# Two heads' scores in the two halves of TensorE's rows, in a macaron block of FFN, ALiBi attention and FFN

## What is computed

```python
def _L0_attn_ref(q, Wq, Wk, Wv, Wo, bo):       # q: 8 x 512 x 256, H = 16 heads of D = 16
    qh, kh, vh = (proj(q, Wq), proj(q, Wk), proj(q, Wv))
    bias = (-slopes)[:, None, None] * abs(pos[None, :] - pos[:, None])
    scores = einsum('bhld,bhsd->bhls', qh, kh) * D ** -0.5 + bias
    attn = softmax(scores, axis=-1)
    out = einsum('bhls,bhsd->bhld', attn, vh)
    return out @ Wo.T + bo
x = x + 0.5 * _L0_ffn_ref(_layernorm(x), ...)
x = x + _L0_attn_ref(_layernorm(x), ...)
x = x + 0.5 * _L0_ffn_ref(_layernorm(x), ...)
```

## Time and profile before

| | |
|---|---|
| Three runs | 908.52, 913.72, 915.49 us; median 913.72 |
| The profiled execution | 917.76 us, of it 915.9 us from first to last instruction |
| Busy (share of the span) | PE 845.7 us (92%), DVE 652.6 (71%), ACT 527.4 (58%), POOL 426.9 (47%) |
| Mean granted TensorE clock | 0.932 |

### The profile page before, as it was taken

One profiled execution on the slowest core, in us unless ns is written; L12 is line 12 of the kernel. 1 busy time (PEld: TensorE's weight loads), 2 busy tenths in 40 slices (PEclk: granted clock), 3 DMA queues, 4 the chain that ended last, 5 costly groups with the idle time before them and its releaser, 6 DMA issues.

```text
span 915.9 us, 15958 instructions
## 1 busy us (share of the span) xinstructions
PE 845.7 (92%) x4672; PEld 578.9 (63%) x4672; DVE 652.6 (71%) x1359; ACT 527.4 (58%) x745; POOL 426.9 (47%) x486
## 2 busy tenths in 40 slices
PE   3899898959999999999999999999999988999988
PEld 2788787835555665665665665665664447888877
DVE  5788777676677677677677677677678706677774
ACT  4444433505668668668668668668666674344443
POOL 0444433522635645645645645645644455334443
PEclk9999999966999999999999999999998998999999
DMA  9220000274382472472472572472572000010001
GB/s 381 82 64 5 0 0 2 48 198 125 86 226 59 117 208 48 114 208 47 117 205 47 116 206 47 119 203 47 122 200 48 2 2 1 25 46 23 23 23 48
DMA packets 37032, 84.48 MB, mean 92 GB/s; under 512 B 3746, under 2 KB 4770, under 8 KB 36818
## 3 DMA queue, kind: packets, MB, share of 16 engines
q1 hardware_dynamic: 36482, 83.45, 34.1%
q10 hardware_dynamic: 512, 0.53, 0.2%
HBM read 45.68 MB, written 38.87 MB: 92 GB/s over the span
## 4 chain that ended last, share of the span: by engine, by line
PE 74%; DVE 10%; issue 6%; DMA 4%; ACT 2%; POOL 2%; ACTq 0%; DVEq 0%; SPq 0%; POOLq 0%
PE ps L969 68%; DVE row_max L882 4%; DMA q_aug<-max_row 3%; DVE xn L731 2%; PE ps L1020 2%; PE ps L981 2%; PE ps L1025 2%; DVE hid L782 1%; POOL hid_r L488 1%; PE ps L1006 1%; PE ps L1030 1%; ACT gated L590 1%; DMA k_aug<-parts_scratch 1%; DMA parts_scratch<-parts 1%; DVE w_max L839 1%
## 5 line engine op out<-in xcount | busy, mean ns | idle before, releaser
L882 DVE TENSOR_REDUCE row_max<-ps 128x1 f32<-128x512 f32 x512 | 341.6, 688 | 130.1 <-PE ps L969 128.4
L678 ACT ACTIVATE probs<-ps 128x1024 f32<-128x1024 f32 x256 | 252.6, 1022 | 101.4 <-PE ps L969 92.3
L555 POOL TENSOR_TENSOR probs<-probs,diag 128x256 f32<-128x256 f32 x256 | 188.1, 737 | 235.2 <-ACT probs L678 234.9
L969 PE MATMUL ps<-k_aug,q_aug 96*128 96x512 f32 x512 | 222.2, 459 | 13.6 <-DVE row_max L882 6.6
L488 POOL TENSOR_TENSOR hid_r<-hid,hid_r 128x512 fp32r<-128x512 f32 x96 | 124.1, 1294 | 184.0 <-ACT hid_r L584 174.5
L969 PE MATMUL ps<-xnt,wgu_r 128*128 128x512 f32 x768 | 183.0, 396 | 11.4 <-issue 9.2
L969 PEld LDWEIGHTS ps<-k_aug,q_aug 96*128 96x128 f32 x512 | 96.2, 195 | 150.3 <-DVE row_max L882 125.2
L969 PEld LDWEIGHTS ps<-xnt,wgu_r 128*128 128x128 f32 x768 | 144.7, 191 | 44.2 <-issue 10.8
L969 PE MATMUL ps<-q_aug,k_aug 98*128 98x512 f32 x512 | 160.0, 406 | 6.7 <-DMA q_aug<-max_row 6.7
L969 PE MATMUL ps<-probs,v_aug 128*32 128x512 f32 x1024 | 142.2, 629 | 0.8 <-POOL probs L555 0.8
L590 ACT ACTIVATE gated<-ps 128x512 f32<-128x512 f32 x96 | 57.6, 600 | 120.4 <-PE ps L969 120.4
(11 more groups left out here) (62 smaller groups left out, 689.7 us busy)
## 6 DMA issues: line engine op xcount, KB each, us to landing
parts_scratch<-parts SPq DMA_DIRECT2D x128, 256.0 KB, 5.8
q_aug<-parts_scratch SPq DMA_DIRECT2D x32, 512.0 KB, 4.8
k_aug<-parts_scratch SPq DMA_DIRECT2D x32, 512.0 KB, 6.5
x_sb<-x_in SPq DMA_DIRECT2D x8, 512.0 KB, 12.6
x_out<-x_sb SPq DMA_DIRECT2D x8, 512.0 KB, 2.6
wgu_i<-w_gate_up SPq DMA_DIRECT2D x2, 768.0 KB, 6.0
k_aug<-k_rows_scratch SPq DMA_DIRECT2D x1, 1088.0 KB
w_att<-w_att SPq DMA_DIRECT2D x1, 1024.0 KB, 11.1
```

The lines of the kernel that those rows point to most:

```text
L555: nc.gpsimd.tensor_tensor(tile, tile, diag[:, n * QH + 2 * pair:n * QH + 2 * pair + 2, :], ALU.mult).then_inc(fixed, 1)
L678: nc.scalar.activation(probs[:, kt % 2, 2 * pair:2 * pair + 2, :], ps[:, at:at + 2, :], ACT.Exp).then_inc(exp_done, 1)
L882: nc.vector.reduce_max(row_max[:, quad % 2, u % TT, u // TT:u // TT + 1], max_bank(b, tile)[0], mybir.AxisListType.X).then_inc(s1_used, 1)
L969: return nc.tensor.matmul(out, lhs, rhs, start=start, stop=stop, **k)
```

## The change

The bias gets six segments instead of eight (twelve pieces of 42 or 43 tokens, two to a segment, its centre between them), products of parts are three instead of four, and slopes are divided by a unit that leaves powers of two (the exponential's scale and the scale of Q carry the unit), so that no bias row needs a low part. A score contracts 62 rows (60 in the first pass). Heads are laid in pairs: `q_aug` and `k_aug` have head i of a pair at partitions 64i to 64i+61. Two successive matmuls of a pair then stand in rows 0 to 63 and 64 to 127 of the array and write different PSUM banks. The first pass orders its tiles so that two neighbours are of the two halves, and `spread_tiles` hands them out in twos.

The maxima of a quad are turned by one transpose (32 columns in, 32 rows out) instead of four; ScalarE only copies them, and SyncE issues the two DMAs (`move_max`), in its own order between the writes and reads of parts. Parts are written and read in two chunks of two quads (DMAs of 512, 256 and four of 384 KB), and the read of a chunk waits until both its quads are done. Three quads of V are placed at once at (3, 7). Fills stand at other steps, weights and lead (24) are new.

```diff
-ROW_BIAS = 4 * D
-ROW_MAX = ROW_BIAS + 4 * NSEG
+NSEG = 6
+HALVES = (0, 43, 85)
+TERMS = 3
+ROW_BIAS = TERMS * D
+ROW_MAX = ROW_BIAS + 2 * NSEG
 ROWS = ROW_MAX + 2
+GROUP = 64
...
 FILLS = {
-    (0, 3): "heads3_prev", (0, 5): "max1", (0, 6): "xt0_next", (0, 7): "xt1_next",
-    (1, 1): "turn1_prev", (1, 2): "qk0_next", (1, 3): "qk1_next", (1, 5): "heads0", (1, 6): "max2",
-    (1, 7): "qk2_next",
-    (2, 1): "qk3_next", (2, 2): "v0_next", (2, 3): "heads1", (2, 5): "max3", (2, 6): "v1_next",
-    (2, 7): "out0_prev",
-    (3, 1): "out1_prev", (3, 3): "heads2", (3, 5): "max0_next", (3, 7): "turn0",
+    (0, 2): "xt0_next", (0, 3): "heads3_prev", (0, 4): "xt1_next", (0, 6): "max1", (0, 7): "turn1_prev",
+    (1, 0): "qk0_next", (1, 2): "qk1_next", (1, 4): "out0_prev", (1, 5): "heads0", (1, 7): "max2",
+    (2, 0): "qk2_next", (2, 2): "qk3_next", (2, 3): "heads1", (2, 4): "out1_prev", (2, 6): "max3",
+    (3, 0): "v0_next", (3, 3): "heads2", (3, 4): "v1_next", (3, 6): "max0_next", (3, 7): "turn0",
 }
-WEIGHT_SCORES, WEIGHT_VALUES = 2, 4.4
-WEIGHTS = {"heads": 2, "max": 2, "turn": 2, "xt": 2, "qk": 6, "v": 6, "out": 6}
-MAX_LEAD = 28
+WEIGHT_SCORES, WEIGHT_VALUES = 0.6, 1.0
+WEIGHTS = {"heads": 0.6, "max": 0.2, "turn": 0.55, "xt": 0.55, "qk": 1.4, "v": 1.7, "out": 1.7}
+MAX_LEAD = 24
...
+            def move_max(b, name):
+                seq, kind, part = fill_parts(b, name)
+                sp.wait_ge(drained, fill_no(b, name) + 1)
+                for i in range(2):
+                    at = i * GROUP + ROW_MAX
+                    sp.dma_start(q_aug[at:at + 2, 2 * part:2 * part + 2, :].bitcast(F32).rearrange("o j (t p) -> o (j t) p", p=P),
+                                 max_row[i * 4 * TT:(i + 1) * 4 * TT, :].bitcast(F32)
+                                 ).then_inc(max_moved, 16)
...
             def turn(b):
+                move_max(b, "max1")
+                if not last(b):
+                    for is_k in range(2):
+                        wait_done(sp, b, f"qk{is_k}_next")
+                        put_parts(0, is_k)
+                move_max(b, "max2")
+                if not last(b):
+                    sp.wait_ge(st_done, b * (NQ * STEPS) + 2 * STEPS)
+                    get_rows(0, CHUNKS * (b + 1) + 1)
+                    for is_k in range(2):
+                        wait_done(sp, b, f"qk{2 + is_k}_next")
+                        put_parts(1, is_k)
+                move_max(b, "max3")
+                if not last(b):
+                    move_max(b, "max0_next")
+                    sp.wait_ge(st_done, b * (NQ * STEPS) + NQ * STEPS)
+                    get_rows(1, CHUNKS * (b + 1) + 2)
...
-                    nc.scalar.copy(max_row[:, :], bank[0:2 * QH, :]).then_inc(drained, 1)
-
-                    act.wait_ge(drained, at + 1)
-                    for i in range(2):
-                        act.dma_start(q_aug[ROW_MAX + i:ROW_MAX + i + 1, part * QH:(part + 1) * QH, :].bitcast(F32),
-                                      max_row[i * QH:(i + 1) * QH, :].bitcast(F32)).then_inc(max_moved, 16)
+                    nc.scalar.copy(max_row[:, :], bank[0:2 * TT * QH, 0:P]).then_inc(drained, 1)
...
-                    for t in tiles:
-                        ins = nc.tensor.transpose(bank[0:2 * QH, t * P:(t + 1) * P], max_in[:, t, :], eye[:])
+                    if halves[0] == 0:
+                        ins = nc.tensor.transpose(bank[0:2 * TT * QH, 0:P], max_in[:].rearrange("p i o j t -> p (i o j t)"), eye[:])
...
-                    h, t = quad * QH + u // TT, u % TT
-                    if u == 0:
-                        pe.wait_ge(aug_done[quad], (seq + 1) * (16 * 2))
+                    pair, t, rows = 2 * quad + u // STEPS, (u % STEPS) // 2, u % 2 * GROUP
+                    if u == 0 and quad % 2 == 0:
+                        pe.wait_ge(aug_done[quad // 2], (seq + 1) * (16 * 4))
...
-                    matmul(bank, q_aug[0:ROW_MAX, h, t * P:(t + 1) * P], k_aug[0:ROW_MAX, h, :],
+                    matmul(bank, q_aug[rows:rows + ROW_MAX, pair, t * P:(t + 1) * P],
+                           k_aug[rows:rows + ROW_MAX, pair, :], True, True).then_inc(s1_done, 1)
...
-                            ins = matmul(ps[:, scores_at + 2 * pair + i, :], k_aug[0:ROWS, h, kt * P:(kt + 1) * P],
-                                         q_aug[0:ROWS, h, :], True, True)
+                            rows = slice(i * GROUP, i * GROUP + ROWS)
+                            ins = matmul(ps[:, scores_at + 2 * pair + i, :],
+                                         k_aug[rows, 2 * n + pair, kt * P:(kt + 1) * P],
+                                         q_aug[rows, 2 * n + pair, :], True, True)
```

More of the change, by code:

```diff
@@ L67, in slopes, with head_of @@
     return np.array([start * start ** i for i in range(H)], dtype=np.float32)
[L70 to L75, removed]
+def head_of(n, j, i):
+    return QH * n + j + 2 * i
+HEADS_IN_ORDER = [head_of(n, j, i) for n in range(NQ) for j in range(2) for i in range(2)]
+SLOPE_UNITS = [float(slopes()[0]), 1.0]
 def tables():
-    s = slopes()
+    s = np.array([slopes()[h] / np.float32(SLOPE_UNITS[h % 2]) for h in range(H)], np.float32)
+    assert np.all(np.frexp(s)[0] == 0.5)
+    bounds = np.array([t * P + x for t in range(TT) for x in HALVES] + [L])
@@ new lines, in tables @@
+    diag = np.zeros((P, 2, H, P), np.float32)
+    for e in range(2):
+        at = e * P + np.arange(P)
+        far = np.abs(at - centre[half[at] // 2])
+        over = (half[at][None, :] == half[at][:, None]) & (far[None, :] > far[:, None])
+        excess = np.where(over, 2.0 * np.abs(at[None, :] - at[:, None]), 0.0)
+        by_head = -slopes().astype(np.float64)[HEADS_IN_ORDER]
+        diag[:, e] = np.exp(by_head[None, :, None] * excess[:, None, :])
+    scale = np.array([D ** -0.5 / np.float32(SLOPE_UNITS[p % 2]) for p in range(P)], np.float32).reshape(P, 1)
@@ L111 @@
+    return {"q_bias": qb, "k_bias": kb, "diag_table": diag, "eye_table": np.eye(P, dtype=np.float32), "q_scale": scale}
+FILLS = {
[4 rows of a table added]
 }
@@ L145, in weight @@
     def weight(n, s, piece):
-        share = LN_SHARE if n == 0 and s < 5 else 1
         if piece.startswith("half"):
-            return WEIGHTS[FILLS[n, s].split("_")[0][:-1]] / 2 * share if (n, s) in FILLS else 0
-        return (WEIGHT_SCORES if piece == "scores" else WEIGHT_VALUES) * share
+            return WEIGHTS[FILLS[n, s].split("_")[0][:-1]] / 2 if (n, s) in FILLS else 0
+        return WEIGHT_SCORES if piece == "scores" else WEIGHT_VALUES
     steps = [(n, s) for n in range(NQ) for s in range(STEPS)]
@@ L157, in spread_tiles @@
             done += weight(n, s, piece)
[L158 removed]
+            until = 2 * int(MAX_TILES // 2 * done / whole + 1e-6)
             out[n, s].append(until - made)
@@ L415, in _ @@
             sp.wait_ge(rows_in, 16 * 2)
[L416 to L428, removed]
@@ new lines, in put_parts, with get_rows @@
+            def put_parts(chunk, is_k):
+                two = d_parts[chunk, is_k, is_k:is_k + 2].rearrange("r i d q t -> (i d q) r t")
+                sp.dma_start(two, parts[chunk][:, is_k, :, :].bitcast(F32)).then_inc(parts_out, 16)
+                again = d_parts[chunk, is_k, 0 if is_k else 2].rearrange("i d q t -> (i d q) t")
+                sp.dma_start(again, parts[chunk][:, is_k, 0, :].bitcast(F32)).then_inc(parts_out, 16)
+            def get_rows(chunk, count):
+                sp.wait_ge(parts_out, PUTS * count)
+                pairs = slice(chunk * NP // CHUNKS, (chunk + 1) * NP // CHUNKS)
+                for i in range(2):
+                    for is_k, aug in ((0, q_aug), (1, k_aug)):
+                        to = aug[i * GROUP:i * GROUP + ROW_BIAS, pairs, :].bitcast(F32)
+                        sp.dma_start(to.rearrange("p q t -> p (q t)"),
+                                     d_parts[chunk, is_k, :, i].rearrange("r d q t -> r d (q t)")
+                                     ).then_inc(aug_done[chunk], 16)
@@ L439, in _ @@
+            for chunk in range(CHUNKS):
                 for is_k in range(2):
-                    wait_done(sp, -1, f"qk{2 * (quad // 2) + is_k}_next")
-                    put_parts(quad, (is_k,))
-                get_rows(quad, quad + 1)
+                    wait_done(sp, -1, f"qk{2 * chunk + is_k}_next")
+                    put_parts(chunk, is_k)
+                get_rows(chunk, chunk + 1)
+            move_max(-1, "max0_next")
             def turn(b):
[L445 to L458, removed]
+                move_max(b, "max1")
[15 more added lines that the diff above has]
+                    get_rows(1, CHUNKS * (b + 1) + 2)
```

150 lines of the change are left out of this document (70 added, 80 removed).

## The result

The changed kernel takes 1194.21 us (median of five, 1188.0 to 1201.82) against 913.45 (908.52 to 915.49): 1.308 times the time, interval 1.303 to 1.312. The forecast was 884 in 838 to 945. The profiled execution took 1188.0 us, of it 1186.2 from first to last instruction, at a mean granted clock of 0.849.

What follows compares the result with a forecast made beforehand. PE sets the pace of the attention stage, VectorE adding 4 us. Terms 55.3 + 6.5 + 0.5 + 2.5 give 64.8 us a sequence against 68.6, hence 884 us in all, range 838 to 945.

Steps and rivals of the forecast that it cites:

- Part 5: Attention stage, rows of q and k: a chunk's reads take about 9 us; 0.5 us of waiting, ends 0 and 3.
- The estimate of the start of the stage: Ahead of the attention stage: longer writes and reads, four tiles fewer running ahead; +1 us in all, -3 to +5.
- Part 1: Scores on PE: two heads side by side in the array, 64 pairs costing 14.4 us a sequence instead of 28.8.
- Part 2: PE's changes of array mode: 77 a sequence instead of 33, at 0.115 us each 8.9 us, making PE 52.7.
- Part 3: DVE's reductions: between pairs passes the larger of PE's work and 1.21 + 0.25 us; 55.3 us a sequence.
- Part 4: The maxima's path to PE at quad borders: waits of 6.5 us a sequence, ends 2 and 12.
- Part 6: PE's clock falling to half around waits for maxima: 2.5 us a sequence, 0 to 7.
- B: Slower side: late maxima at each quad's border and half clock take all the gain; 960 us, chance 0.13.
- C: The array's halves don't run side by side: 74 to 75 us a sequence, about 960 us; chance 0.10.
- A: Waits for maxima don't come: 52 to 57 us a sequence remain; 805 us at 55, chance 0.14.
- D: A draw: mode changes at the upper end with 10 us of waits and clock; 905 to 920 us, chance 0.13.
- Wrong by most would make me: Named ahead: waits at every border sized from one loaded landing, and mode changes costing otherwise between rows than columns.

Runs made afterwards that it cites:

- Experiment 1: The changed kernel with its reads of q and k rows walked by 16 channels first instead of 3 terms: 980.66 us, ratio 1.072.
- experiment 4: The kernel before with both passes contracting only the first 66 rows, 926.17 us, and with only the first 62, 1018.42 us.
- experiment 5: Changed kernel, channel-first reads, second pass not waiting for maxima: 938.7 us. Instead with quad-wise reads, earlier maxima: 946.59; that with ScalarE issuing maxima's transfers: 1006.31.
- experiment 2: The changed kernel with its three-step reads started by quads: 1060.72 us, ratio 1.162; with reads also walked by channels, 982.86 us.
- experiment 3: The changed kernel with channel-first reads, both heads of a pair reading the rows of the first half: 1218.93 us.

## Why the prediction was wrong, point by point

**Part 5, rows of q and k, is the step that failed.** It took two reads of 512 KB at 6.5 us, scaled them by bytes to 9 for a chunk and put 0.5 us of waiting a sequence, ends 0 and 3. The bytes were right, the rate was not the same: the new transfers begin with 3 steps instead of 16. A chunk took 24 us, PE waited 23 a sequence (186.8 less the first 25.0, over seven), and the clock fell behind it. No end of the range held this, since no end changed the rate. Experiment 1 gives 213.6 of the 281 us to that line. The estimate of the start of the stage (+1 us, up to +5) fell by the same step: the first scores stand at 241.6 instead of 211.8, and at 215.4 in experiment 1.

With the reads mended, the order alone gives 980.7, also above the range. Its sequence of 74.4 us beside the forecast's 64.8:

- *Part 1, pairs.* 64 x 0.225 = 14.4 forecast, 64 x 0.336 = 21.5 measured: +7.1. The mechanism was right (3 to 8 ns apart), the size was off. The estimate beside it, 18.7, from the factor for four row tiles of the Trainium skill, TensorE: Matmul & The Clock Gate, Part 3, was nearer.
- *Part 2, changes of mode.* 77 counted, 77 in the trace; price 0.13 on average (experiment 4). The pieces other than pairs took 34.9 in experiment 1 instead of 29.5, so 5.4 for 8.9: -3.5. Why 77 changes cost less than their price here wasn't followed; a part may be in the pairs. Together PE's own 52.7 became 56.4.
- *Part 3, VectorE.* The form of the rule was right, its constant wasn't: 1.46 us between pairs forecast, 1.87 needed. With the clock it is 9.5 us a sequence (the rest of 74.4), where 2.6 and 2.5 stood: +4.4. In the trace late second tiles are 3.3 of it, the clock at most 3.5 (7.0 us at half in this sequence), waits for copies and for `probs` 1.1; 1.6 or more stay open.
- *Part 4, maxima.* 6.5 forecast, 5.9 measured (46.9 us in eight sequences), removed by experiment 5 for 42 us. Right, and by quad too: 0.5 at quad 0, 1.2 at 1, 2.3 at 2, 1.9 at 3, where 1.0, 1.2, 2.3 and 3.2 stood before the deduction. Only the loaded queue at `max3` didn't show.
- *Not in the sum at all*: 2.6 us a sequence in which PE waits for VectorE's `xn`, since `xt0` stands at (0, 2):

```profile
520.52 0.66 PE L1018 MATMUL ps<-eye,xn 128*128 128x128 f32 x4 [2.57 <-DVE xn L767]
```

- *Part 6, clock.* 2.5 forecast, end 7. In experiment 1 133 us at half, 99 more than before, at most 50 lost or 6 a sequence: inside its ends. (Half of 3.4 us is 1.7, not the 1.25 of the sum; by 1.7 the term is 3.4.)

3.7 + 4.4 + 2.6 - 0.6 (maxima) - 0.5 (the reads' term) = 9.6, from 64.8 to 74.4. So with the reads mended several misses add up; the largest are the pairs (+7.1), the exchange with the clock (+4.4) and `xn` (+2.6), against -3.5 for the changes of mode.

Of the rivals none was it. B's mechanism, late maxima at every border, exists, but in the changed kernel 187 us stand at the tiles and 45 at the scores, 11.2 of these ahead of the stage's first; maxima came later than B's 3.5 us, by 9, only in experiment 2. C was refuted. A needed waits that don't come, and D allowed 10 us a sequence for waits and clock, where the waits for K alone took 23. B and C both gave 960, so a range that ended at 945 left out the figures of both, not only their upper halves.

The signs named ahead: pairs' starts under 0.12 us apart, seen; the piece behind a pair at 0.3 to 0.4, seen (0.33); maxima's idle 6 to 8 a sequence, most at quads 2 and 3, 5.9 in experiment 1 and most there; clock 0.50 inside the stage, seen. Not seen: a sequence of 62 to 68 us (102.7, and 74.4 in experiment 1), and VectorE's idle time of about 10 us before reductions (52.2, and 24.1). None of them looked at the reads. "Wrong by most would make me" named two things, and neither was it.

## What to carry to other kernels

Before a transfer is scaled by its bytes, look at the outermost step of both its patterns: a layout that puts a small extent first (3 terms) ran at 81 GB/s where the same bytes ran at 164, and what was issued behind it came late too. A matmul of half the rows pays only as a pair, and here a pair cost 0.33 us against 0.46 and then bound the order of work to the pace of two banks; what is gained at the array must be looked for again at the engine that empties PSUM. A stall on PE is paid again where the clock then falls, so a transfer with only five or six steps of slack should be priced with it.

## What the runs showed of the hardware

- A low clock can outlast the waits that it follows. With all scores in one half of the rows it stayed at 0.50 for 17 to 31 us with PE nearly always busy (30.70 of 30.70 us from 323.70 on, experiment 3); with 62 rows in the kernel before, for 109 us with PE busy for 104 (experiment 4). With pairs the stretches inside the stage were 3.4 to 10.2 us (experiment 1). Why isn't shown.
- At full level the profile of before shows 0.95 and those of the experiments 1.00, with the same price of a tile (0.23 us); the profiled run took 917.8 us, the medians beside the experiments are 913.7 to 914.1.
- Three DMA engines moved 81 GB/s, 27 each; sixteen moved 164, some 10 each (experiment 1). Five times the engines gave twice the rate.
- Two transfers of 8 KB let PE go on 1.9 us after the second one's issue when they stood ahead of the reads (changed kernel, 480.77), 8.6 us after it behind three-engine reads (experiment 2), and 6.2 us after it from a queue of their own beside wide reads (experiment 5).
- A matmul of 62 rows that follows another in the same half costs 0.28 us (0.57 for two), in the whole array 0.23.
